# An adaLN block with delta-rule attention and routed experts: half of each inverse root from one ScalarE activation

## The chip, the cores and the metric

The kernel runs on one core of one Trainium2 chip. The metric is the device time of one execution in microseconds (us); lower is better. The core has five engines with a queue of instructions each: TensorE (PE) multiplies matrices, VectorE (DVE), ScalarE (ACT) and GpSimd (POOL) work element by element on 128 partitions, SyncE (SP) issues DMAs. Each engine works its own list in order, and engines wait for each other by semaphores. ScalarE holds one table of functions at a time; where the next activation needs another, a load of a table (`ACT_TABLE_LOAD`) stands in front of it.

## The reference

```python
def step(S, inp):                                    # 256 times, for 16 batches x 16 heads
    qt, kt, vt, at, bt = inp
    Sd = at[..., None, None] * S
    u = vt - jnp.einsum('bhk,bhkv->bhv', kt, Sd)
    Sn = Sd + bt[..., None, None] * kt[..., None] * u[:, :, None, :]
    return (Sn, jnp.einsum('bhk,bhkv->bhv', qt, Sn))
...
k = k * jax.lax.rsqrt(jnp.sum(k * k, -1, keepdims=True) + 1e-12)      # root of the keys
o = o * jax.lax.rsqrt(jnp.mean(o * o, -1, keepdims=True) + 1e-6)      # root of the outputs
...
h = _layernorm(x, axis=-1) * (1 + ca) + sa           # root of the variances, 1e-5
x = x + ga * attention(h)
h = _layernorm(x, axis=-1) * (1 + cb) + sb           # root of the variances, 1e-5
x = x + gb * experts(h)                              # best of 8 experts per row, silu(a) * g @ w2
```

x is 16 x 256 x 128, all in fp32, with heads of 8 values. Every inverse square root in it is one of three kinds: of the variances of rows (layer norm), of the squared length of each key, of the mean square of each output.

## The kernel before, in words

Time is cut into two slices of 128 steps, and batches into two halves of 8. Sequences (batch, head) lie on the 128 partitions of a half `h`; the recurrence is worked in 64 chunks of 4 steps.

Front (0 to 81 us of the profile): VectorE takes statistics of x and scales the rows (`normalise`), TensorE turns and projects them in eight blocks, ScalarE evacuates each block (`shift`, `evacuate`), SP and POOL move them by DMA onto the partitions of their sequences, and VectorE prepares the first slice: unit keys, decay factors, a triangular solve per chunk (`key_norms`, `unit_keys`, `decay_factors`, `key_products`, `substitute`).

Scan (81 to 345 us): VectorE runs four instructions per chunk and half (L1479, L1485, L1492, L1498). Between them it works, one step at a time, through a Python generator, `between()`: the preparation of the second slice, then the first slice's output norm, second layer norm, router and sort. Every `yield` of the generator gives way to one instruction of the scan; `after_chunk(n)` holds it until chunk n. ScalarE's own work for the same things is tied to chunk numbers too. POOL makes products of queries and states, which TensorE sums.

Experts (345 to 543 us): 46 tiles of 128 sorted rows, 23 for each slice. Tile g's weights are copied by ScalarE (`copy_w1`, L1219), TensorE computes the hidden rows (L718) and the outputs (L733), ScalarE applies Silu (L1206), VectorE the gate (`gate_u`, L1695). The second slice's output norm, attention projection, layer norm, router and sort are done beside the first slice's tiles, at fixed g (`F_ATTEND`, `F_ROOT`, `F_TURN`, `F_ROUTE`). POOL scatters the second slice's rows (L868) before tile 23 can start, and scatters each tile's result (L921).

An inverse root has two engines. VectorE makes the argument with its epsilon (`variances` L1309, `key_norms` L1350, `sums_of_squares` L1507) and posts `root_in`; ScalarE's `root` takes the square root by `ACT.Sqrt` (L947) and posts `root_out`; VectorE takes the reciprocal and one Newton step (`rsqrt` L1290 to L1293; for the keys, whose argument, root and result lie in PSUM, `unit_keys` L1357 to L1361 with a copy to SBUF). `settle` makes each wait for the one before. There are ten such roots: four of variances on 128x16 values, four of keys on 128x128, two of outputs on 128x256. An eleventh `ACT.Sqrt` at L1231, whose result nobody uses, stands before the first copies of weights.

Of the kernel before, what the change touches and what calls it, by code (L numbers as in the profile page):

```python
# [12 lines left out]
P = 128  # L13
# [5 lines left out]
def adaln_block(nc, x, Wq, Wk, Wv, Wo, Wbet, Wf, norm_w, router_w, router_b, w1, w2, c, wmod, out):  # L19
# [66 lines left out]
    with ExitStack() as ctx:  # L86
# [56 lines left out]
        ve = sb("ve", [P, NT])  # L143
        sd = sb("sd", [P, NT])
# [618 lines left out]
        def _(pool):  # L763
# [89 lines left out]
            def place_rows(s):  # L853
                for h in range(NHALF):
                    if s == 0:
                        pool.wait_ge(sem("prod_ready", h), NG // 2 + 1)
                    else:
                        pool.wait_ge(sem("sqo_used"), 2)
# [71 lines left out]
        def _(act):  # L930
# [13 lines left out]
            def root(dst, src):  # L944
                roots[0] += 1
                act.wait_ge(sem("root_in"), roots[0])
                act.activation(dst, src, ACT.Sqrt).then_inc(sem("root_out"), 1)  # L947
# [49 lines left out]
            def key_roots(h, s):  # L997
                vectors = bank_vectors(h, s)
                root(vectors[1], vectors[0])

            root(sd[:, :], ve[:, :])
# [4 lines left out]
            root(sd[:, :], ve[:, :])  # L1006
# [90 lines left out]
            def squares(s, h):  # L1097
# [7 lines left out]
                act.activation(SQO[s][h], K_[h][:, s * P:(s + 1) * P, :], ACT.Square).then_inc(sem("sqo"), 1)  # L1105
# [21 lines left out]
            def rows(k):  # L1127
# [3 lines left out]
                if k == 4:  # L1131
                    act.wait_ge(sem("sqo_used"), 2)
# [19 lines left out]
            for n in range(NCH):  # L1152
# [30 lines left out]
                if n == AT_ROOT:  # L1183
                    root(sm[:, 3, :], sm[:, 2, :])
                if n == AT_ROWS:
                    root(sd[:, :], ve[:, :])
# [44 lines left out]
            act.activation(sd[:, :], ve[:, :], ACT.Sqrt)  # L1231
# [5 lines left out]
            root(sm[:, 3, :], sm[:, 2, :])  # L1237

            for g in range(G):
# [9 lines left out]
                if g == F_ROOT:  # L1249
                    root(sd[:, :], ve[:, :])  # L1250
# [5 lines left out]
        def _(dve):  # L1256
# [29 lines left out]
            def rsqrt(var, sroot, y, t):  # L1286
# [3 lines left out]
                yield from settle(dve.reciprocal(y, sroot))  # L1290
                yield from settle(dve.tensor_tensor(t, y, y, ALU.mult))
                yield from settle(dve.scalar_tensor_tensor(out=t, in0=t, scalar=-0.5, in1=var, op0=ALU.mult, op1=ALU.mult))
                dve.scalar_tensor_tensor(out=y, in0=t, scalar=1.5, in1=y, op0=ALU.add, op1=ALU.mult).then_inc(sem("roots_ready"), 1)  # L1293
# [11 lines left out]
            def variances():  # L1305
                for t in range(NT):
                    last = dve.bn_aggr(mv[:, t, :], st[:, t, :])
                yield from settle(last)
                yield from ask_root(dve.tensor_scalar(ve[:, :], mv[:, :, 1], LN_EPS, None, ALU.add))  # L1309
# [8 lines left out]
            def normalise(s):  # L1318
# [4 lines left out]
                now(rsqrt(ve[:, :], sd[:, :], yy[:, :], y2[:, :]))  # L1323
# [19 lines left out]
            def key_norms(h, s):  # L1343
# [5 lines left out]
                yield from settle(dve.tensor_reduce(n2, slice_rows(K_[h], s), AX_X, ALU.add))  # L1349
                yield from ask_root(dve.tensor_scalar(n2, n2, K_EPS, None, ALU.add))  # L1350

            def unit_keys(h, s):
                beta, a, n2, rt, rn, t_, d2, d3 = slice_vectors(h, s)
                n2, rt, rn, a = bank_vectors(h, s)
                count = roots[0]
                dve.wait_ge(sem("root_out"), count)
                yield from settle(dve.reciprocal(rn, rt))  # L1357
                yield from settle(dve.tensor_copy(d2, rn))
                yield from settle(dve.tensor_tensor(t_, rn, d2, ALU.mult))
                yield from settle(dve.scalar_tensor_tensor(out=t_, in0=t_, scalar=-0.5, in1=n2, op0=ALU.mult, op1=ALU.mult))  # L1360
                dve.scalar_tensor_tensor(out=rn, in0=t_, scalar=1.5, in1=rn, op0=ALU.add, op1=ALU.mult).then_inc(sem("roots_ready"), 1)  # L1361
                yield
                dve.wait_ge(sem("roots_ready"), count)
# [136 lines left out]
            def sums_of_squares(s, h):  # L1500
# [3 lines left out]
                if h == 1:  # L1504
                    last.then_inc(sem("sqo_used"), 1)
                    dve.wait_ge(sem("sqo_used"), s + 1)
                    yield from ask_root(dve.tensor_scalar(ms, ms, 1.0 / HD, O_EPS, ALU.mult, ALU.add))  # L1507
# [121 lines left out]
            def first_slice_rows():  # L1629
# [11 lines left out]
                yield from rsqrt(*(sm[:, i, :] for i in (2, 3, 4, 5)))  # L1641
# [170 lines left out]
```

## Time and profile before

| | us |
|---|---|
| median of 3 runs (517.99 to 519.32) | 518.33 |
| profiled execution, first to last instruction (span; the profile gives no other time of it) | 543.5 |
| VectorE busy in it | 414.1 (76%) |
| TensorE busy | 389.4 (72%) |
| GpSimd busy | 276.2 (51%) |
| ScalarE busy | 272.0 (50%) |

The busy share is a mean over stages with different limits. The page puts reciprocals of the keys (L1357) at 3.8 us for 4, reciprocals of the outputs (L1290) at 3.5 us for 2, and loads of ScalarE's table at 1283 ns each, 20 of them. In a row of a timeline stand start, duration, engine, line, operation, output and input tile with shapes, the count of instructions merged into the row, and in brackets the idle time before it and what ended it. A start that follows the end of the row before at once means that nothing was waited for. The mean granted TensorE clock was 0.840 of full speed.

### The profile page before, as it was taken

What the parts mean: (1) busy time and instruction counts of PE and PEld (TensorE: products, weight loads), DVE (VectorE), ACT (ScalarE), POOL (GpSimd) and SP (SyncE); (2) the same over time, 40 slices, a digit from 0 to 9 for tenths busy, and PEclk for the clock granted to TensorE, in tenths of its full rate; (3) what the DMA queues carried; (4) which work ended last, traced back from release to release, by engine and by line L of the source; (5) the groups of instructions that cost most, each with busy time, mean ns of one, the idle gap of its engine ahead of it and who ended that gap; (6) DMA issues with size and microseconds to landing.
All of it is one profiled execution on the core that took longest, in us unless ns stands there. A gap on an engine that the chain in (4) does not pass through costs nothing. (4 is left out here: it accounts for less than half of the span.)

```text
span 543.5 us, 8910 instructions
## 1 busy us (share of the span) xinstructions
PE 389.4 (72%) x2643; PEld 352.1 (65%) x2643; DVE 414.1 (76%) x1196; ACT 272.0 (50%) x600; POOL 276.2 (51%) x323
## 2 busy tenths in 40 slices
PE   2957555969677799450968664879999338999980
PEld 1322115969677699450968663879999238999980
DVE  5679999996999978999998996685957013548733
ACT  2688749663144244554555461453755026555620
POOL 1174329699999674537379375002223743232430
PEclk9988775868977787975889776789999759999996
DMA  8367859900000009203100012024130111233205
GB/s 206 60 70 122 117 105 144 113 1 1 0 2 1 0 8 378 82 0 50 29 2 0 1 35 60 20 39 99 41 107 25 55 54 40 77 91 94 60 29 159
DMA packets 50205, 35.01 MB, mean 64 GB/s; under 512 B 10992, under 2 KB 46608, under 8 KB 50032
## 3 DMA queue, kind: packets, MB, share of 16 engines
q1 hardware_dynamic: 47152, 29.07, 27.5%
q0 software_dynamic: 3008, 5.40, 3.2%
q8 instruction: 22, 0.36, 0.3%
q14 instruction: 23, 0.19, 0.1%
HBM read 15.26 MB, written 10.27 MB: 47 GB/s over the span
## 5 line engine op out<-in xcount | busy, mean ns | idle before, releaser
L570 PE MATMUL bank<-prod_o,ID 128*128 128x128 f32 x512 | 85.5, 336 | 41.3 <-POOL prod_o L287 18.0
L921 POOL DMA_INDIRECT placed_y<-Q,place x46 | 44.1, 958 | 126.0 <-ACT Q L1226 60.6
L570 PEld LDWEIGHTS bank<-prod_o,ID 128*128 128x128 f32 x512 | 79.9, 246 | 43.1 <-POOL prod_o L287 18.8
L718 PE MATMUL bank<-Q,p 128*128 128x128 f32 x736 | 96.5, 280 | 0.0
L718 PEld LDWEIGHTS bank<-Q,p 128*128 128x128 f32 x736 | 91.6, 196 | 0.1
L280 POOL TENSOR_TENSOR prod_o<-Q,ST 128x1024 f32<-128x1024 f32 x28 | 62.5, 2231 | 42.4 <-PE bank L574 29.1
L1063 ACT ACTIVATE p<-S,GAM 128x64 f32<-128x64 f32 x126 | 47.6, 410 | 70.6 <-DVE S L1498 68.0
L1219 ACT ACTIVATE p<-big 128x1024 f32 x46 | 48.5, 1057 | 54.8 <-PE bank L718 36.9
L1498 DVE TENSOR_REDUCE S<-p 128x64 f32<-128x320 f32 x126 | 55.4, 474 | 6.5 <-ACT p L1063 6.0
L1485 DVE TENSOR_REDUCE U<-p 128x32 f32<-128x288 f32 x128 | 52.7, 439 | 0.2 <-DVE p L1479 0.2
L1479 DVE TENSOR_TENSOR p<-S,bank 128x256 f32<-128x256 f32 x128 | 49.2, 407 | 0.7 <-ACT bank L1058 0.7
L1492 DVE TENSOR_TENSOR p<-U,bank 128x256 f32<-128x256 f32 x126 | 47.3, 408 | 0.6 <-DVE U L1485 0.6
L537 PE MATMUL bank<-ph,WP 128*128 128x512 f32 x48 | 32.1, 822 | 18.1 <-ACT ph L959 14.0
L287 POOL TENSOR_TENSOR prod_o<-PD,U 128x128 f32<-128x128 f32 (+1 forms) x112 | 41.5, 405 | 0.0
L1695 DVE TENSOR_TENSOR S<-S,bank 128x512 f32<-128x512 f32 x31 | 21.3, 686 | 25.4 <-PE bank L718 12.5
L574 PEld LDWEIGHTS bank<-prod_o,ID 128*128 128x128 f32 x256 | 37.4, 223 | 3.8 <-issue 3.8
L574 PE MATMUL bank<-prod_o,ID 128*128 128x128 f32 (+3 forms) x256 | 37.1, 293 | 3.4 <-issue 3.4
L1688 DVE COPY Q<-bank 128x128 f32<-128x128 f32 x46 | 13.2, 287 | 33.0 <-PE bank L706 23.9
L868 POOL DMA_INDIRECT sorted_h<-X,pos x32 | 30.8, 963 | 14.1 <-issue 9.1
L733 PE MATMUL bank<-big,S 128*128 x248 | 34.3, 283 | 3.6 <-DVE Q L1702 2.0
L733 PEld LDWEIGHTS bank<-big,S 128*128 128x128 f32 x248 | 30.9, 196 | 4.6 <-issue 4.6
L537 PEld LDWEIGHTS bank<-ph,WP 128*128 128x128 f32 x48 | 11.3, 250 | 32.2 <-ACT ph L959 17.4
(225 smaller groups left out, 786.7 us busy)
## 6 DMA issues: line engine op xcount, KB each, us to landing
big<-in_L_ffn_w_dram SPq DMA_DIRECT2D x1, 4096.0 KB, 13.1
big<-big SPq DMA_DIRECT2D x16, 192.0 KB, 4.5
Q<-sorted_h SPq DMA_DIRECT2D x46, 64.5 KB, 2.0
sorted_h<-ZERO SPq DMA_DIRECT2D x2, 1472.0 KB, 16.4
X<-in_L_attn_x_dram SPq DMA_DIRECT2D x8, 256.0 KB, 4.8
big<-big SPq DMA_DIRECT2D x16, 128.0 KB, 4.9
X<-Q SPq DMA_DIRECT2D x32, 64.0 KB, 2.4
K<-placed_y SPq DMA_DIRECT2D x8, 256.0 KB, 3.0
```

The costliest lines, as they stand in the source:

```text
L280: engine.tensor_tensor(slot[:, 0:HD, :, :, :], q, states.unsqueeze(3).broadcast_to(full), ALU.mult)
L570: pe.matmul(ps, ID[:, :], prod_o[:, k % 2, i, :], start=(i == 0), stop=False, skip_group_check=True)
L574: m = pe.matmul(o4, ID[:, :], r4, start=False, stop=(d == C - 1), skip_group_check=True)
L718: m = pe.matmul(bank[(1, 6)[g % 2] + k][:, c * P:(c + 1) * P], W1E[g % 2][:, f:f + P], XST[:, g % 3, :], start=True, stop=True)
L733: m = pe.matmul(bank[3][:, 0:D], GU[g % 3][:, c * P:(c + 1) * P], W2[:, bass.ds(expert, 1), c, :], start=(c == 0), stop=(c == FC - 1))
L921: pool.indirect_dma_start(placed_y[g // NF], bass.IndirectOffsetOnAxis(ap=place[:, g:g + 1], axis=0), YS[:, g % YR, :], None).then_inc(sem ...
L1063: act.activation(p2[h][:, :, :, C], S_[h][:, n % SR, :, :], ACT.Copy, scale=GAM[h][:, n:n + 1])\
L1219: act.activation(W1E[g % 2].unsqueeze(1), W1[:, bass.ds(expert, 1), :], ACT.Copy).then_inc(sem("w1_copied"), 1)
L1479: dve.tensor_tensor(p1[h][:, n % UR, :, :, 0:HD], s_, w, ALU.mult).then_inc(sem("seq_w", h), 1)
L1485: dve.tensor_reduce(U_[h][:, n % VR, :, :], p1[h][:, n % UR, :, :, :], AX_X, ALU.add)\
L1492: dve.tensor_tensor(p2[h][:, :, :, 0:C], u, k, ALU.mult).then_inc(sem("state_in", h), 1)
L1498: dve.tensor_reduce(S_[h][:, (n + 1) % SR, :, :], p2[h][:, :, :, :], AX_X, ALU.add).then_inc(sem("s_ready", h), 1)
```

## The change

ScalarE no longer gives a square root but `Abs_reciprocal_sqrt` of 4 v + 4 eps, which is half of the inverse root. VectorE keeps a Newton step written for the half: t = -4 half half, t = (v + eps) t, y = (t + 3) half. The epsilon operations, the reciprocals and the keys' copy go. The outputs' 1/8 moves into ScalarE's Square. The reduction itself (or the last aggregation) now posts `root_in`, and two waits on `sqo_used` become waits on a count of `root_in`. The unused `ACT.Sqrt` at L1231 goes. For the keys, `half` lies in SBUF (`d2`), argument and result in PSUM. The diff leaves out the two tiles that go and further calls of `root` and `rsqrt` with their new arguments.

```diff
@@ -855,7 +853,7 @@
                     else:
-                        pool.wait_ge(sem("sqo_used"), 2)
+                        pool.wait_ge(sem("root_in"), 2 * NHALF + 2 * NTIME + 1)
@@ -941,10 +939,11 @@
-            def root(dst, src):
+            def root(half, src, eps):
+
...
                 act.wait_ge(sem("root_in"), roots[0])
-                act.activation(dst, src, ACT.Sqrt).then_inc(sem("root_out"), 1)
+                act.activation(half, src, ACT.Abs_reciprocal_sqrt, scale=4.0, bias=4.0 * eps).then_inc(sem("root_out"), 1)
@@ -995,15 +994,14 @@
             def key_roots(h, s):
-                vectors = bank_vectors(h, s)
-                root(vectors[1], vectors[0])
-
-            root(sd[:, :], ve[:, :])
+                root(slice_vectors(h, s)[6], bank_vectors(h, s)[0], K_EPS)
+
+            root(yy[:, :], mv[:, :, 1], LN_EPS)
...
             evacuate(1)
-            root(sd[:, :], ve[:, :])
+            root(yy[:, :], mv[:, :, 1], LN_EPS)
@@ -1102,7 +1100,8 @@
                         act.wait_ge(sem("q_decayed", hh), 2)
-                act.activation(SQO[s][h], K_[h][:, s * P:(s + 1) * P, :], ACT.Square).then_inc(sem("sqo"), 1)
+                act.activation(SQO[s][h], K_[h][:, s * P:(s + 1) * P, :], ACT.Square, scale=HD ** -0.5)\
+                    .then_inc(sem("sqo"), 1)
@@ -1228,13 +1227,12 @@
-            act.activation(sd[:, :], ve[:, :], ACT.Sqrt)
...
                 squares(1, h)
-            root(sm[:, 3, :], sm[:, 2, :])
+            root(sm[:, 4, :], sm[:, 2, :], O_EPS)
@@ -1283,14 +1281,13 @@
-            def rsqrt(var, sroot, y, t):
+            def rsqrt(var, eps, half, y, t):
...
                 dve.wait_ge(sem("root_out"), count)
-                yield from settle(dve.reciprocal(y, sroot))
-                yield from settle(dve.tensor_tensor(t, y, y, ALU.mult))
-                yield from settle(dve.scalar_tensor_tensor(out=t, in0=t, scalar=-0.5, in1=var, op0=ALU.mult, op1=ALU.mult))
-                dve.scalar_tensor_tensor(out=y, in0=t, scalar=1.5, in1=y, op0=ALU.add, op1=ALU.mult).then_inc(sem("roots_ready"), 1)
+                yield from settle(dve.scalar_tensor_tensor(out=t, in0=half, scalar=-4.0, in1=half, op0=ALU.mult, op1=ALU.mult))
+                yield from settle(dve.scalar_tensor_tensor(out=t, in0=var, scalar=eps, in1=t, op0=ALU.add, op1=ALU.mult))
+                dve.scalar_tensor_tensor(out=y, in0=t, scalar=3.0, in1=half, op0=ALU.add, op1=ALU.mult).then_inc(sem("roots_ready"), 1)
@@ -1305,8 +1302,7 @@
                     last = dve.bn_aggr(mv[:, t, :], st[:, t, :])
-                yield from settle(last)
-                yield from ask_root(dve.tensor_scalar(ve[:, :], mv[:, :, 1], LN_EPS, None, ALU.add))
+                yield from ask_root(last)
@@ -1346,21 +1342,12 @@
                 dve.wait_ge(sem("ksq"), NHALF * s + h + 1)
-                yield from settle(dve.tensor_reduce(n2, slice_rows(K_[h], s), AX_X, ALU.add))
-                yield from ask_root(dve.tensor_scalar(n2, n2, K_EPS, None, ALU.add))
+                yield from ask_root(dve.tensor_reduce(n2, slice_rows(K_[h], s), AX_X, ALU.add))
...
                 n2, rt, rn, a = bank_vectors(h, s)
-                count = roots[0]
-                dve.wait_ge(sem("root_out"), count)
-                yield from settle(dve.reciprocal(rn, rt))
-                yield from settle(dve.tensor_copy(d2, rn))
-                yield from settle(dve.tensor_tensor(t_, rn, d2, ALU.mult))
-                yield from settle(dve.scalar_tensor_tensor(out=t_, in0=t_, scalar=-0.5, in1=n2, op0=ALU.mult, op1=ALU.mult))
-                dve.scalar_tensor_tensor(out=rn, in0=t_, scalar=1.5, in1=rn, op0=ALU.add, op1=ALU.mult).then_inc(sem("roots_ready"), 1)
-                yield
-                dve.wait_ge(sem("roots_ready"), count)
+                yield from rsqrt(n2, K_EPS, d2, rn, t_)
@@ -1502,9 +1489,7 @@
                 if h == 1:
-                    last.then_inc(sem("sqo_used"), 1)
-                    dve.wait_ge(sem("sqo_used"), s + 1)
-                    yield from ask_root(dve.tensor_scalar(ms, ms, 1.0 / HD, O_EPS, ALU.mult, ALU.add))
+                    yield from ask_root(last)
@@ -1638,14 +1623,14 @@
                 yield from after_chunk(AT_ROOT)
-                yield from rsqrt(*(sm[:, i, :] for i in (2, 3, 4, 5)))
+                yield from rsqrt(sm[:, 2, :], O_EPS, sm[:, 4, :], sm[:, 4, :], sm[:, 5, :])
...
                 yield from after_chunk(AT_ROWS)
-                yield from rsqrt(ve[:, :], sd[:, :], yy[:, :], y2[:, :])
+                yield from rsqrt(mv[:, :, 1], LN_EPS, yy[:, :], yy[:, :], y2[:, :])
```

## Rows read from the trace of the kernel before

**Rows 1.** Busy time of each engine in four stretches (us, instructions), clock, DMA.
```profile
33.00:81.50 48.50, 30.15 (x61) 9.79 (x59) 44.94 (x81) 35.42 (x64) 22.28 (x21) 0.82 0.64 101
...
130.00:180.00 50.00, 39.18 (x264) 38.71 (x263) 49.97 (x117) 16.50 (x54) 49.30 (x48) 0.80 0.00 1
...
380.00:419.00 39.00, 37.05 (x325) 36.06 (x324) 29.40 (x117) 22.95 (x37) 9.58 (x10) 1.00 0.18 57
419.00:444.00 25.00, 6.59 (x47) 5.94 (x45) 2.23 (x8) 2.91 (x4) 16.28 (x17) 0.66 0.19 59
```

**Rows 2.** Timeline of VectorE: the first root of variances.
```profile
10.69 0.17 DVE L1309 TENSOR_SCALAR ve<-RT 128x16 f32<-128x16 f32 x1
11.22 0.25 DVE L1290 RECIPROCAL yy<-sd 128x16 f32<-128x16 f32 x1 [0.36 <-ACT sd L947]
```

**Rows 3.** Timeline of VectorE: second root of variances, first root of keys.
```profile
28.93 0.25 DVE L1290 RECIPROCAL yy<-sd 128x16 f32<-128x16 f32 x1 [5.84 <-ACT sd L947]
...
33.29 1.23 DVE L1349 TENSOR_REDUCE bank<-K 128x128 f32<-128x1024 f32 x1 [1.29 <-ACT K L980]
34.55 0.30 DVE L1350 TENSOR_SCALAR bank<-bank 128x128 f32<-128x128 f32 x1
35.25 0.96 DVE L1357 RECIPROCAL bank<-bank 128x128 f32<-128x128 f32 x1 [0.40 <-ACT bank L947]
...
36.57 0.29 DVE L1359 TENSOR_TENSOR sm<-bank,sm 128x128 f32<-128x128 f32 x1
```

**Rows 4.** Timeline of ScalarE: the second root of keys.
```profile
53.04 1.28 ACT L947 ACT_TABLE_LOAD   x1
55.67 0.26 ACT L947 ACTIVATE bank<-bank 128x128 f32<-128x128 f32 x1 [1.35 <-DVE bank L1350]
```

**Rows 5.** Timelines of POOL, TensorE and VectorE: from the front into the scan.
```profile
81.50 6.04 POOL L827 TENSOR_TENSOR prod_o<-Q,K 128x1024 f32<-128x1024 f32 x4 [7.62 <-DVE X L1436]
...
87.60 10.64 PE L590 MATMUL bank<-prod_o,ID 128*128 128x128 f32 x64 [10.60 <-POOL prod_o L827]
...
128.74 0.26 DVE L1418 TENSOR_TENSOR sm<-sm,bank 128x96 f32<-128x96 f32 x1 [4.15 <-PE bank L603]
```

**Rows 6.** Timeline of VectorE: reciprocals inside the scan, and what follows each.
```profile
136.98 0.95 DVE L1357 RECIPROCAL bank<-bank 128x128 f32<-128x128 f32 x1
137.84 0.39 DVE L1485 TENSOR_REDUCE U<-p 128x32 f32<-128x288 f32 x1
...
243.52 1.75 DVE L1290 RECIPROCAL sm<-sm 128x256 f32<-128x256 f32 x1
245.18 0.36 DVE L1479 TENSOR_TENSOR p<-S,bank 128x256 f32<-128x256 f32 x1
...
274.44 0.61 DVE L1309 TENSOR_SCALAR ve<-RT 128x16 f32<-128x16 f32 x1
```

**Rows 7.** Timeline of ScalarE, where the experts start.
```profile
345.92 1.28 ACT L1231 ACT_TABLE_LOAD   x1
...
351.30 1.06 ACT L1105 ACTIVATE X<-K 128x1024 f32<-128x1024 f32 x1
...
354.40 1.28 ACT L1206 ACT_TABLE_LOAD   x1
```

**Rows 8.** Timeline of VectorE, the same stretch.
```profile
353.64 0.29 DVE L1507 TENSOR_SCALAR sm<-sm 128x256 f32<-128x256 f32 x1
...
355.01 1.74 DVE L1290 RECIPROCAL sm<-sm 128x256 f32<-128x256 f32 x1
356.79 0.42 DVE L1291 TENSOR_TENSOR sm<-sm 128x256 f32<-128x256 f32 x1
...
358.17 0.69 DVE L1695 TENSOR_TENSOR S<-S,bank 128x512 f32<-128x512 f32 x1
```

**Rows 9.** Timelines of TensorE and ScalarE: a late transfer, and a standstill.
```profile
368.75 2.05 PE L619 MATMUL bank<-ph,X 128*128 128x128 f32 x16 [1.02 <-DMA X<-Q]
...
441.44 1.06 ACT L1219 ACTIVATE p<-big 128x1024 f32 x1 [12.03 <-remote]
```

More of the change, by code:

```diff
@@ L142, in adaln_block @@
         mv = RT[:, 992:1024].rearrange("p (t a) -> p t a", t=NT)
-        ve = sb("ve", [P, NT])
-        sd = sb("sd", [P, NT])
         yy = sb("yy", [P, NT])
@@ L1131, in rows @@
                 if k == 4:
-                    act.wait_ge(sem("sqo_used"), 2)
+                    act.wait_ge(sem("root_in"), 2 * NHALF + 2 * NTIME + 1)
                 act.activation(H2[s][q // 2][:, q % 2 * 4:q % 2 * 4 + 4, 0:D], BACK_BANKS[s][q][:, :].rearrange("p (n d) -> p n d", n=4), ACT.Copy)\
@@ L1183, in _ @@
                 if n == AT_ROOT:
-                    root(sm[:, 3, :], sm[:, 2, :])
+                    root(sm[:, 4, :], sm[:, 2, :], O_EPS)
                 if n == AT_ROWS:
-                    root(sd[:, :], ve[:, :])
+                    root(yy[:, :], mv[:, :, 1], LN_EPS)
                 if n in AT_STATS:
@@ L1236, in _ @@
                 squares(1, h)
-            root(sm[:, 3, :], sm[:, 2, :])
+            root(sm[:, 4, :], sm[:, 2, :], O_EPS)
             for g in range(G):
@@ L1249, in _ @@
                 if g == F_ROOT:
-                    root(sd[:, :], ve[:, :])
+                    root(yy[:, :], mv[:, :, 1], LN_EPS)
                 if g == NF - 1:
@@ L1322, in normalise @@
                 now(variances())
-                now(rsqrt(ve[:, :], sd[:, :], yy[:, :], y2[:, :]))
+                now(rsqrt(mv[:, :, 1], LN_EPS, yy[:, :], yy[:, :], y2[:, :]))
                 scale(s, tile, XN[s], "xn_ready", range(HB if s else NT))
@@ L1740, in _ @@
                 if g == 0:
-                    now(rsqrt(*(sm[:, i, :] for i in (2, 3, 4, 5))))
+                    now(rsqrt(sm[:, 2, :], O_EPS, sm[:, 4, :], sm[:, 4, :], sm[:, 5, :]))
                 if g - 1 in F_ATTEND:
@@ L1753, in _ @@
                 if g == F_ROOT + 1:
-                    now(rsqrt(ve[:, :], sd[:, :], yy[:, :], y2[:, :]))
+                    now(rsqrt(mv[:, :, 1], LN_EPS, yy[:, :], yy[:, :], y2[:, :]))
                     scale(1, second_tile, XNB, "xn2_ready", range(NT // 2))
```

## The prediction

> **What bounds the kernel now.** I read the busy time by stretch first, because the page's busy shares mix stages. VectorE is busy 44.94 of 48.5 us in the second part of the front and 49.97 of 50 in the middle of the scan; POOL is busy 49.30 of the same 50; between 380 and 419 us TensorE is the full one (37.05 of 39) [rows 1]. So an instruction that leaves VectorE should shorten the span up to about 345 us, unless a wait already stands behind it, and should be worth little beside the experts' tiles. Then I went through VectorE's timeline for its idle times, as each is a place where an earlier saving can stop. Up to 345 us those that matter are: 5.84 us for ScalarE's second root and 1.29 us for the keys' squares [rows 3], and 4.15 us at 128.74 for TensorE's sums of key products [rows 5]. Last I followed the two other engines at the start of the experts [rows 7, 8] and looked for what stops all of them at once [rows 9].
>
> **The front.** First root of variances: without L1309 the argument is ready 10.89 - 10.69 = 0.20 us earlier (its 0.17 us and a gap), and the reciprocal goes (0.25 us and a gap of 0.04) [rows 2]. The Newton step is three instructions before and after, on operands of the same shape, so it costs the same. 0.20 + 0.29 = 0.49 us, and all that follows (turning, projecting, moving the keys) hangs on these rows. Second root of variances: VectorE waits 5.84 us for ScalarE, which is in its own queue behind the projections, so L1309 is worth nothing; the reciprocal's 0.29 us comes back, but is lost at 33.29, where VectorE waits 1.29 us for the squares of the keys [rows 3]. Counted: 0.
>
> First root of keys: L1350 takes 34.55 to about 34.88, 0.33 us; from the reciprocal to L1359 it is 36.57 - 35.25 = 1.32 us, which holds the reciprocal (0.96) and the copy that goes [rows 3]. What remains is a product, and the two instructions of the step. Saved 1.65 us. The second root of keys in the front has the same five instructions, so 1.65 us again, if its root is there in time. ScalarE waited 1.35 us for VectorE before it, with the table long loaded (53.04 to 54.32) [rows 4]. VectorE now has the argument 0.49 + 1.65 + 0.33 = 2.47 us sooner, so ScalarE is the later one, at about 54.3 less 0.5; VectorE wants the result some 3 us after that. No loss. The front gives 0.49 + 3.30 = 3.79 us.
>
> Whether this reaches the scan is the first choice I had to make. At 128.74 VectorE waits for TensorE, and the chain behind that is TensorE's sums of query products from 87.60 on, begun by POOL's products at 81.50, which waited 7.62 us for VectorE's last substitution [rows 5]. So the wait at 128.74 moves with the front: 3.79 us pass through. But what is saved between 82 and 128 us (the third root of keys, the fourth's epsilon) only makes the wait of 4.15 us longer. Counted: 0.
>
> **The scan.** Here the generator puts each removed instruction between two of the recurrence, and they overlap a little: the reciprocal of 0.95 us moves its successor by 137.84 - 136.98 = 0.86 us, the one of 1.75 us by 245.18 - 243.52 = 1.66 us [rows 6]. Fourth root of keys: 0.86 and a copy, for which I take 0.2 (it is of the shape of L1350, 0.30 us in [rows 3], less the same overlap of 0.1): 1.06 us. First root of outputs: 1.66 and an epsilon operation of 0.2 (0.29 alone in [rows 8], less 0.1): 1.86 us. Third root of variances: L1309 took 0.61 us there [rows 6], and a short reciprocal, 0.25 less 0.1: I count 0.5. ScalarE's waits in this part lead back to TensorE and POOL, and these back to chunks that VectorE had finished; so all of it passes. 1.06 + 1.86 + 0.5 = 3.42 us.
>
> POOL is nearly as full as VectorE from 130 to 180 us [rows 1], which speaks against this; the bounds are 0 (POOL sets the pace) and 3.42. I take 3.42, because the run of POOL ends in an idle stretch that waits for TensorE, not for POOL's own work.
>
> **The start of the experts.** The unused Sqrt at L1231 goes, with its 1.28 us load [rows 7], but a load has to stand somewhere: it now comes before the root itself, after the square that ends at 351.30 + 1.06 = 352.36. A load is not held back by the wait of the activation that it is for (1.35 us of waiting stand behind the load of [rows 4]), so it runs from 352.36 to 353.65. VectorE's last sum ends at about 353.61 (before L1507 at 353.64) and no longer needs the epsilon operation, so the root starts at about 353.68, against 353.96: nearly hidden, and 0.28 us earlier. VectorE then needs 3 x 0.46 = 1.38 us instead of 1.78 + 3 x 0.46 (from L1290 to L1291 is 356.79 - 355.01 = 1.78) [rows 8]. The tile's gate at L1695 waits for the step and for Silu, whose load at 354.40 [rows 7] moves by 0.28. Gate: 358.17 less about 2.0 us, 356.1 to 356.2. The scaling of outputs, its transfer and the projection for which TensorE waited 1.02 us at 368.75 [rows 9] follow it. I take 2.0; the bounds are 1.02 (only that wait goes) and 2.06 (1.78 + 0.28). With the cover gone, a load costs 1.28 us there: were it issued only with the root, the sum would be 2.0 - 1.3 = 0.7.
>
> A rule to weigh against this: the row has the load at 1.28 us, and the engine busy again at once behind it [rows 7]. The Trainium skill, "ScalarE: Activation LUTs", section "What ACT_TABLE_LOAD costs", charges a switch at about 2.66 us, a load and a drain of 1.38 us. With the drain the moved load would end 1.4 us behind the sum, and 0.6 us would be left of the 2.0; the trace shows no such drain, and I go by the trace.
>
> **Beside the tiles.** The last root of variances gives at most 0.49 us by the first one's rows; TensorE is full there, and I count 0.2.
>
> **What could be added.** The activation itself: 0.26 us for Sqrt on 128x128 [rows 4]; the new function is not in the trace. Square on 1024 elements takes 1.06 us [rows 7] and Sqrt on 128 0.26: an activation goes by its elements. Below, the new one costs the same; above, I allow twice that for each of the five on the path, 5 x 0.26 = 1.3 us. I take the same. The count of loads: Copy, Identity and Square run between a Sqrt and the next load in this trace, and I take it that they stand in the new function's table too. The Square's scale costs nothing by the form of the instruction.
>
> **Sum.** 3.79 + 3.42 + 2.0 + 0.2 = 9.4 us. The profiled span would be 543.5 - 9.4 = 534.1. That span is 25.2 us longer than the median of 518.33; I can't place the difference, but the standstill below is as long. The instructions saved are the same either way, so I take 9.2 from the median, a little less for gaps that open: 509.1 us.
>
> **The rivals.** A. Another engine takes over inside the scan: POOL at 49.30 of 50 us [rows 1]. Then the front's 3.79 us and the last 2.2 us stay, less some, and the scan's 3.4 goes: 518.3 - 5.8 = 512.5. For it: POOL's share; against it: the 7.62 us that POOL waited for VectorE [rows 5].
>
> B. The standstill moves. Between 419 and 444 us, while POOL issues the second slice's scatters, TensorE, VectorE and ScalarE are busy for 6.59, 2.23 and 2.91 of 25 us [rows 1], and ScalarE waits 12.03 us for nothing that the profile can name [rows 9]. If this depends on where in its list each engine is, 20 instructions fewer can change it. Worse: one more such wait of 12.03 us on the path, and the kernel is slower, 518.3 - 9.2 + 12.0 = 521.1; it decides from 9.2 us on. Better: the some 8 us of tiles that now run after it fit under POOL's scatters: 509.1 - 8 = 501.
>
> C. The new function's table lacks Copy, Identity or Square. Then up to ten more loads of 1.28 us, 12.8 us on ScalarE, of which I would expect a third on the path: 509.1 + 4.3 = 513.4. All ten on the path would make 521.9.
>
> D. The gain is there only in part because the moved load is not hidden and the second stretch of the front has a new wait: 509.1 + 1.3 + 1 = 511.4. This lies in my forecast's own range of 506.5 to 511.5.
>
> **Chances.** Forecast with D 0.63, A 0.16, B worse 0.06, B better 0.10, C 0.05. The range from 503.5 to 514.0 holds the forecast, A, most of C and a part of B better. 0.3% is 1.6 us, the least that can be told from no change: faster 0.90, same 0.04, slower 0.06.
>
> **What would show it.** In the changed profile: 20 loads of tables as before; no reciprocal of 0.96 or 1.74 us; the key products' wait (4.15 us before) at about 125.0 and longer, some 5.6 us; the scan's end 7.2 us earlier; the first gate of the experts 9.2 us earlier than 358.17; the last root's load covered by the sum of squares. I am wrong if VectorE shows new idle time between 33 and 81 us or for POOL in the scan, if ScalarE's loads are more than 20, or if the first gate is early and the end is not, which would be the standstill.

## The result, and the profile after

The changed kernel takes 512.34 us (median of 4 runs, 511.5 to 515.14), the kernel before beside it 518.83 us (4 runs, 517.99 to 521.38). The ratio is 0.9887, 95% interval 0.9848 to 0.9926: 5.9 us faster, from 3.8 to 7.9 (the medians alone differ by 6.5). I had forecast 9.2 us less and 509.1 us.

The profiled execution of the changed kernel has a span of 509.7 us (its time 511.5), that of before 543.5. These 34 us are not the change. The windows of the changed kernel (window, length, busy us of TensorE, its weight loads, VectorE, ScalarE and POOL with instruction counts, granted clock, DMA share, GB/s) answer to [rows 1]:

```profile
33.00:80.50 47.50, 28.44 (x60) 9.54 (x58) 44.30 (x75) 35.31 (x64) 22.68 (x21) 0.82 0.73 104
130.00:180.00 50.00, 39.57 (x261) 39.12 (x260) 49.97 (x108) 16.59 (x54) 49.02 (x47) 0.79 0.00 1
...
419.00:444.00 25.00, 23.16 (x199) 22.34 (x198) 11.07 (x34) 15.13 (x20) 17.22 (x18) 1.00 0.39 112
```

The last row shows that this execution has no standstill. Every later comparison was run on one of three other chips, where each kernel shows it and takes some 27 us more (the kernel before 545.1 to 546.3 us). There I compare times only by the ratio to the kernel before beside them. Traces can be set side by side across these chips: from 201 to 214 us, where VectorE never waits, two kernels on two chips run alike to 0.01 us.

The first two rows show what didn't happen: in the scan's stretch VectorE starts nine instructions fewer, of which the change removed only two there (a reciprocal and a copy), and is busy for the same 49.97 of 50 us. Over the whole execution it went from 414.1 to 411.0 us, 3.1 us, while the reciprocals, epsilon operations and copies that go were busy for 12.4 us by the groups of the kernel before (3.8 + 3.5 + 1.0 of reciprocals, 1.2 + 1.1 + 0.6 of epsilons, 1.2 of copies). So something else got longer. The groups by form name most of it (busy us, mean ns of one):

```profile
L1288 DVE SCALAR_TENSOR_TENSOR sm<-sm 128x128 f32<-128x128 f32 x2 | 3.3, 1668 | 0.4 <-ACT sm L946 0.4
L1290 DVE SCALAR_TENSOR_TENSOR bank<-XN 128x128 f32<-128x128 f32 x2 | 3.0, 1484 | 0.0
L1289 DVE SCALAR_TENSOR_TENSOR sm<-bank,sm 128x128 f32<-128x128 f32 x2 | 0.6, 282 | 0.0
```

Three steps of the same form and size; the two whose inputs both lie in SBUF take five to six times as long in the mean. The mean hides a spread: of the eight steps of this kind (L1288 and L1290 at four roots of keys) three are long, 3.00, 1.62 and 1.35 us, and five take 0.28 to 0.34. The three long ones account for 5.1 of the 9.3 us that are missing. Another 2.3 us are in older instructions with two SBUF inputs, which the change left alone: the products of keys with keys (`multiply_pairs`, big<-K, "the pairs" below) went from 5.3 to 6.4 us busy, and the substitutions of the triangular solve (L1421 and L1423) from 35.1 to 36.3. In the scan, instructions overlap by about 0.1 us each, which a sum over groups counts twice. The timelines of VectorE and of POOL, put side by side at the third root of keys and then at the second and fourth, say why:

```profile
94.23 3.00 DVE L1288 SCALAR_TENSOR_TENSOR sm<-sm 128x128 f32<-128x128 f32 x1
...
97.48 0.28 DVE L1289 SCALAR_TENSOR_TENSOR sm<-bank,sm 128x128 f32<-128x128 f32 x1
...
98.04 0.28 DVE L1290 SCALAR_TENSOR_TENSOR bank<-sm 128x128 f32<-128x128 f32 x1
...
92.56 2.59 POOL L794 TENSOR_TENSOR X<-big,sm 128x1024 f32<-128x1024 f32 x1
95.11 1.96 POOL L842 TENSOR_TENSOR Q<-Q,sm 128x1024 f32<-128x1024 f32 x1
```

```profile
59.16 1.62 DVE L1290 SCALAR_TENSOR_TENSOR bank<-XN 128x128 f32<-128x128 f32 x1
...
137.19 1.35 DVE L1290 SCALAR_TENSOR_TENSOR bank<-XN 128x128 f32<-128x128 f32 x1
...
58.55 2.07 POOL L811 TENSOR_TENSOR big<-K,sm 128x1024 f32<-128x1024 f32 x1 [9.64 <-DVE X L1423]
...
136.16 2.22 POOL L278 TENSOR_TENSOR prod_o<-Q,ST 128x1024 f32<-128x1024 f32 x1
```

VectorE's step ends at 97.23, 60.78 and 138.54; POOL's instruction ends at 97.07, 60.62 and 138.38. Each time it is 0.16 us, so the step can finish only when POOL is through. No wait stands in the profile, only a long duration: that a row which follows the one before at once has waited for nothing, as said ahead of the rows, does not hold for such an instruction. In the kernel before, all instructions of a root of keys read at most one operand from SBUF, since argument and root lay in PSUM. The change put `half` into SBUF.

The Trainium skill, "SBUF — State Buffer", section "Who interferes with whom", states this: a VectorE instruction with two SBUF inputs and a GpSimd instruction that reads SBUF share a read path, whoever issues first holds it, and the other blocks fully. The rows above agree. My prediction did not weigh it.

VectorE's other rows at the places of the prediction, and ScalarE's at the start of the experts:

```profile
28.77 0.17 DVE L1288 SCALAR_TENSOR_TENSOR y<-yy 128x16 f32<-128x16 f32 x1 [6.58 <-ACT yy L946]
...
33.10 1.23 DVE L1345 TENSOR_REDUCE bank<-K 128x128 f32<-128x1024 f32 x1 [1.57 <-ACT K L979]
...
126.84 0.26 DVE L1405 TENSOR_TENSOR sm<-sm,bank 128x96 f32<-128x96 f32 x1 [1.81 <-PE bank L601]
...
241.66 0.41 DVE L1288 SCALAR_TENSOR_TENSOR sm<-sm 128x256 f32<-128x256 f32 x1
...
243.03 0.40 DVE L1290 SCALAR_TENSOR_TENSOR sm<-sm 128x256 f32<-128x256 f32 x1
...
343.46 0.42 DVE L1288 SCALAR_TENSOR_TENSOR sm<-sm 128x256 f32<-128x256 f32 x1
...
344.86 0.69 DVE L1680 TENSOR_TENSOR S<-S,bank 128x512 f32<-128x512 f32 x1
```

```profile
340.07 1.06 ACT L1103 ACTIVATE X<-K 128x1024 f32<-128x1024 f32 x1
341.15 1.28 ACT L946 ACT_TABLE_LOAD   x1
342.44 0.42 ACT L946 ACTIVATE sm<-sm 128x256 f32<-128x256 f32 x1
342.88 1.28 ACT L1205 ACT_TABLE_LOAD   x1
```

The last root of outputs takes no longer by the new function (0.42 us, as by Sqrt), and tables are loaded 20 times, as before. From the last square's end to the first gate it is 344.86 - 341.13 = 3.73 us, against 358.17 - 352.36 = 5.81 in [rows 7, 8].

### The profile page after: what moved, and what is told of

It reads as the page before. It is cut to its first block, busy times and chain, and to the rows that moved or that the text cites. A ratio compares the mean times of both kernels' runs of the same rounds, so it can differ in the third digit from the quotient of the medians.

```text
span 509.7 us, 8886 instructions
## 1 busy us (share of the span) xinstructions
PE 382.6 (75%) x2643; PEld 346.9 (68%) x2643; DVE 411.0 (81%) x1172; ACT 272.2 (53%) x599; POOL 277.2 (54%) x323
## 4 chain that ended last, share of the span: by engine, by line
DVE 39%; PE 38%; issue 8%; POOL 6%; DMA 4%; ACT 2%; SPq 2%; ACTq 0%; POOLq 0%; DVEq 0%
PE bank L716 11%; PE bank L568 7%; PE bank L731 5%; PE bank L588 5%; DVE U L1472 5%; DVE S L1485 4%; DVE p L1479 4%; DVE p L1466 4%; DVE big L1421 3%; DVE X L1423 3%; PE bank L572 2%; POOL placed_y L919 1%; PE bank L601 1%; DVE big L1391 1%; PE bank L535 1%
## 5 line engine op out<-in xcount | busy, mean ns | idle before, releaser
L568 PE MATMUL bank<-prod_o,ID 128*128 128x128 f32 x512 | 84.4, 333 | 39.9 <-ACT K L1091 16.9
L568 PEld LDWEIGHTS bank<-prod_o,ID 128*128 128x128 f32 x512 | 78.7, 242 | 41.4 <-issue 17.6
L716 PE MATMUL bank<-Q,p 128*128 128x128 f32 x736 | 94.8, 277 | 0.0
L716 PEld LDWEIGHTS bank<-Q,p 128*128 128x128 f32 x736 | 89.8, 193 | 0.2
L572 PEld LDWEIGHTS bank<-prod_o,ID 128*128 128x128 f32 x256 | 37.2, 223 | 0.0
L588 PE MATMUL bank<-big,ID 128*128 128x128 f32 (+3 forms) x192 | 31.8, 340 | 1.0 <-POOL big L825 1.0
```

The source lines that it names most:

```text
L568: pe.matmul(ps, ID[:, :], prod_o[:, k % 2, i, :], start=(i == 0), stop=False, skip_group_check=True)
L572: m = pe.matmul(o4, ID[:, :], r4, start=False, stop=(d == C - 1), skip_group_check=True)
L588: m = pe.matmul(ps, ID[:, :], t4[:, :, :, k], start=(k == 0), stop=(k == HD - 1))
L716: m = pe.matmul(bank[(1, 6)[g % 2] + k][:, c * P:(c + 1) * P], W1E[g % 2][:, f:f + P], XST[:, g % 3, :], start=True, stop=True)
```

## The experiments

Each row of this table is from 5 to 12 timed executions, beside 17 of the kernel before on the same chip.

| kernel | chip | median (range), us | kernel before | ratio, 95% interval |
|---|---|---|---|---|
| changed | first | 539.22 (538.63 to 541.78) | 546.02 | 0.9889 (0.986 to 0.9918) |
| keys padded | first | 543.83 (543.18 to 545.65) | 546.02 | 0.9967 (0.9951 to 0.9983) |
| half twice | first | 541.11 (538.34 to 542.49) | 546.02 | 0.9908 (0.9876 to 0.994) |
| keys as before | second | 539.4 (538.03 to 541.68) | 546.32 | 0.9876 (0.985 to 0.9902) |
| outputs padded | second | 544.76 (543.73 to 546.58) | 546.32 | 0.9978 (0.9959 to 0.9996) |
| new order | second | 539.75 (536.96 to 542.11) | 546.32 | 0.986 (0.983 to 0.9889) |
| half twice, new order | second | 538.43 (536.24 to 542.11) | 546.32 | 0.9848 (0.9809 to 0.9888) |
| changed | third | 539.84 (538.86 to 540.83) | 545.06 | 0.9906 (0.9885 to 0.9928) |
| half twice, new order | third | 536.95 (536.77 to 541.56), 5 runs | 545.06 | 0.986 (0.9834 to 0.9885) |
| before, new order | third | 544.93 (540.3 to 548.09) | 545.06 | 0.9998 (0.9975 to 1.002) |
| root's table early | third | 538.89 (538.35 to 540.59) | 545.06 | 0.9897 (0.9874 to 0.992) |

**The kernel before, and the changed one, on one chip.** 

> The kernel before once more, unchanged, for its trace. Theory S (the two standstills of its first trace, about 4 us at 334 to 338 and about 22 us at 420 to 443, belong to that one execution): the span comes out near 517 us, and from 419 to 444 us TensorE is busy for far more than 6.6 us. Rival (they belong to the kernel, and the change removes them): the span is near 543 us again.

> The changed kernel unchanged, as the point of comparison for the two beside it. Expected 511 to 513 us, a ratio of 0.985 to 0.991 to the kernel before; key steps of VectorE at L1288 and L1290 again stretched from 0.28 us to 1.3 to 3.0 us in three of eight places.

The control took 546.25 us, span 544.5, so my theory S was wrong. But the changed kernel has the standstill here as well (its execution took 541.78 us), so its rival was wrong too: the change does not remove it. Four of the eight steps are long this time, 1.62, 1.08, 1.18 and 1.35 us. Both kernels stand still between 419 and 444 us: in order, the changed one and the one before:

```profile
419.00:444.00 25.00, 7.76 (x41) 7.30 (x41) 2.92 (x10) 3.87 (x5) 14.60 (x16) 0.60 0.18 55
```
```profile
419.00:444.00 25.00, 6.65 (x56) 6.11 (x54) 2.90 (x10) 2.94 (x4) 17.18 (x18) 0.75 0.20 62
```

So the standstill is a matter of the chip or the execution, not of the kernel, and the gain is the same with it and without (0.9887, and 0.9889 in the table). These two traces, of one chip, give the account by place. The starts of the same VectorE instructions, in us:

| VectorE starts | before | changed | keys padded | keys as before |
|---|---|---|---|---|
| first squares of keys are summed | 33.57 | 33.62 | 33.33 | 33.17 |
| first key product (its root is done) | 37.83 | 36.28 | 37.84 | 37.43 |
| decay factors (after the pairs) | 43.20 | 42.64 | 42.55 | 42.45 |
| second key product | 62.84 | 61.34 | 63.68 | 61.48 |
| third key product | 99.48 | 98.06 | 101.65 | 98.12 |
| chunk 16 of the scan | 156.57 | 155.76 | 159.80 | 155.55 |
| chunk 40, behind the outputs' root | 250.20 | 247.43 | 249.57 | 246.08 |
| chunk 48, behind the variances' root | 278.23 | 274.35 | 276.69 | 272.99 |
| last chunk | 342.48 | 338.92 | 341.92 | 336.07 |
| first gate | 359.19 | 353.33 | 356.31 | 350.31 |

Two things in these columns belong to the execution and not to the kernel. The trace of the changed kernel is of the slowest of its six executions (541.78 us), that of the keys as before of the fastest (538.03). And ahead of the last chunk, from 328 to 340 us, VectorE stands idle several times for nothing that the profile can name, in one piece for 3.56, 1.78, 5.30 and 1.80 us.

**Keys padded.** The new form stays, and an epsilon operation, a reciprocal and a copy whose results nobody reads come back:

```diff
+                yield from settle(dve.tensor_scalar(rn, n2, K_EPS, None, ALU.add))
+                yield from settle(dve.reciprocal(rn, n2))
+                yield from settle(dve.tensor_copy(rn, n2))
                 yield from rsqrt(n2, K_EPS, d2, rn, t_)
```

> The changed kernel, with what it took from VectorE per root of keys put back as work that nobody uses: an epsilon operation, a reciprocal and a copy on 128x128 from PSUM to PSUM, 1.6 us each time, ahead of the steps. The outputs and the variances keep the new form. My prediction's terms: 1.65 twice and 1.06, so 4.4 us slower than the changed kernel. Theory P (most of the keys' saving was lost in waiting for POOL's reads): 1 to 2.5 us slower, because padding takes up time in which VectorE would wait anyway.

It is 4.6 us slower than the changed kernel, as the prediction's 4.4 had it, and not the 1 to 2.5 us of the other theory. On this run alone my account of the keys would have passed as confirmed. Its trace is less clear: it is 4.0 us behind the changed kernel's at chunk 16, but only 2.1 at chunk 40, as two waits of VectorE for ScalarE, near 200 and 215 us, take 3.05 us and nothing in it, 3.69 and 1.49 in the other.

**Half twice.** ScalarE writes the keys' half into SBUF and into the bank, so that each step reads one operand of SBUF at most:

```diff
+                act.activation(bank_vectors(h, s)[1], bank_vectors(h, s)[0], ACT.Abs_reciprocal_sqrt, scale=4.0, bias=4.0 * K_EPS)\
+                    .then_inc(sem("half_in"), 1)
...
-                yield from settle(dve.scalar_tensor_tensor(out=t, in0=half, scalar=-4.0, in1=half, op0=ALU.mult, op1=ALU.mult))
+                yield from settle(dve.scalar_tensor_tensor(out=t, in0=half, scalar=-4.0, in1=twin, op0=ALU.mult, op1=ALU.mult))
```

> ScalarE writes the half of the keys' inverse root twice, to PSUM and to SBUF, so that none of VectorE's three steps on keys has two inputs in SBUF. Theory P (such an instruction can't run beside a POOL instruction that reads SBUF, and waits to its end): L1288 at 94 us falls from 3.0 us to 0.28, L1290 at 59 and 137 us from 1.6 and 1.35 to 0.29; of that the one at 94 us lies in the shadow of the wait for the key products, the one at 59 us is lost again on the pairs of keys behind it, which have two inputs in SBUF, so the time falls by 0 to 1.5 us against the changed kernel. Rival Q (the stretch is POOL's and TensorE's pace, or a wait that the trace hides in the duration): the three stay stretched and the time is the same. ScalarE pays 4 x 0.26 us.

The steps are short now, at the place where one took 1.62 us, and the pairs behind them take the wait over (62.98: 3.54 us for three that take 2.14 undisturbed, at 63.61 in the keys as before):

```profile
60.05 0.29 DVE L1292 SCALAR_TENSOR_TENSOR XN<-XN,bank 128x128 f32<-128x128 f32 x1
60.37 0.29 DVE L1293 SCALAR_TENSOR_TENSOR XN<-bank,XN 128x128 f32<-128x128 f32 x1
60.69 0.29 DVE L1294 SCALAR_TENSOR_TENSOR bank<-XN,bank 128x128 f32<-128x128 f32 x1
61.02 1.92 DVE L1356 TENSOR_TENSOR K<-big,bank 128x1024 f32<-128x1024 f32 x1
62.98 3.54 DVE L1396 TENSOR_TENSOR big<-K 128x768 f32<-128x768 f32 x3
```

All twelve steps at the four roots take 0.27 to 0.30 us. The mechanism is confirmed and the cure is not: 541.11 against 539.22 us, with overlapping ranges, where I expected 0 to 1.5 us less. Freed at one instruction, VectorE stops at the next that reads two operands from SBUF while POOL works.

**Keys as before.** The whole of the keys' old form, in the changed kernel:

```diff
+                yield from ask_root(dve.tensor_scalar(n2, n2, K_EPS, None, ALU.add))
...
+                yield from settle(dve.reciprocal(rn, rt))
+                yield from settle(dve.tensor_copy(d2, rt))
+                yield from settle(dve.tensor_tensor(t_, rt, d2, ALU.mult))
+                yield from settle(dve.scalar_tensor_tensor(out=t_, in0=t_, scalar=-4.0, in1=n2, op0=ALU.mult, op1=ALU.mult))
...
```

> The changed kernel with VectorE's work on the roots of the keys put back as it was, at the four places where a root of keys is taken: ScalarE writes its half into the bank alone, VectorE adds the epsilon in an operation of its own, takes a reciprocal (which nothing reads), copies the half, and the three instructions of the step each read at most one operand from SBUF. Variances and outputs keep the new form. By my prediction's terms this gives back 1.65 + 1.65 + 1.06 = 4.4 us, so the kernel is 4.4 us slower than the changed one. By the shared-read theory (the changed form saves instructions at the keys, but makes two of the three steps read two operands from SBUF, and these stand still beside POOL) it is 0 to 1 us slower only. A padded kernel that kept the two-operand steps and added the instructions was 4.6 us slower than the changed one: if this one is too, the placing of the operands is worth nothing.

Ratio 0.9876 against 0.9889 of the changed kernel: the same. By the two intervals the undone kernel is 0.7 us faster, give or take 2.1, so the 4.4 us of the forecast are excluded and a gain of about 1.4 us is not. So all that the change did to the keys, three VectorE instructions of six gone at four places, gained nothing that can be measured. The timeline of VectorE at the first root, in the changed kernel and in this one, and of the padded one at the second:

```profile
35.26 0.33 DVE L1288 SCALAR_TENSOR_TENSOR sm<-sm 128x128 f32<-128x128 f32 x1 [0.41 <-ACT sm L946]
...
36.28 1.92 DVE L1351 TENSOR_TENSOR K<-big,bank 128x1024 f32<-128x1024 f32 x1
38.24 4.37 DVE L1391 TENSOR_TENSOR big<-K 128x768 f32<-128x768 f32 x3
```
```profile
35.13 0.97 DVE L1353 RECIPROCAL bank<-bank 128x128 f32<-128x128 f32 x1 [0.40 <-ACT bank L946]
...
37.43 1.91 DVE L1360 TENSOR_TENSOR K<-big,bank 128x1024 f32<-128x1024 f32 x1
39.38 3.04 DVE L1400 TENSOR_TENSOR big<-K 128x768 f32<-128x768 f32 x3
```
```profile
61.47 2.18 DVE L1290 SCALAR_TENSOR_TENSOR bank<-XN 128x128 f32<-128x128 f32 x1
63.68 1.92 DVE L1355 TENSOR_TENSOR K<-big,bank 128x1024 f32<-128x1024 f32 x1
```

The changed kernel has its root 1.15 us sooner, though it summed its squares 0.45 us later, and the pairs end at 42.61 against 42.42 us: of 1.6 us gained 0.26 are left. The pairs are instructions with two SBUF inputs (2.14 us for the three undisturbed), and POOL's weighing of values lies across them, which itself is held up by them, by the timeline of POOL in the changed kernel and in this one:

```profile
38.48 3.12 POOL L794 TENSOR_TENSOR X<-big,sm 128x1024 f32<-128x1024 f32 x1
```
```profile
37.88 2.53 POOL L794 TENSOR_TENSOR X<-big,sm 128x1024 f32<-128x1024 f32 x1
```

At the second root the step at 59.69 takes 1.62 us and gives the gain back at once (61.34 against 61.48), at the third two steps take 1.08 and 1.18 us (98.06 against 98.12), and at the fourth a lead of 0.8 us (139.48 against 140.26) is gone by chunk 16; what took it there was not tried. The padded kernel pays for both: the added instructions and the long step, 2.18 us in the last fence, at its second root.

**Outputs padded.** An epsilon operation and a reciprocal, whose results nobody reads, stand ahead of both roots of outputs:

```diff
+                yield from settle(dve.tensor_scalar(sm[:, 5, :], sm[:, 2, :], O_EPS, None, ALU.add))
+                yield from settle(dve.reciprocal(sm[:, 5, :], sm[:, 2, :]))
...
```

> The changed kernel with an epsilon operation and a reciprocal on 128x256 elements, whose results nothing reads, ahead of both roots of outputs (one in the scan, one at the start of the experts). By my prediction's terms 1.86 + 2.0 = 3.9 us slower than the changed kernel. If the first is swallowed in the scan by POOL's pace (the prediction's rival A), 2.0 us slower; if the table load moved by the change really hides the second, the same 2.0 stays in the first alone, about 1.9 to 2.2.

By the ratios it is 0.9978 - 0.9889 = 0.0089 of 546.3, 4.9 us slower than the changed kernel (5.4 slower than the keys as before beside it); the prediction had 3.9. In its trace, against the changed kernel, it is 0.92 us ahead at chunk 36 and 0.88 behind at chunk 40, 1.8 us for the scan's root, and from the last sum of squares to the first gate it is 357.58 - 353.02 = 4.56 us against 353.33 - 350.85 = 2.48, 2.1 us. Both terms stand at their place. The 1.0 us beyond them is within the intervals, which allow 1.9 either way.

**Two changes of order.** VectorE takes the first half's decay factors ahead of its pairs, and POOL weighs the second values before it waits for the first keys' factors; alone in the changed kernel, with the half twice, the latter again, and alone in the kernel before:

```diff
-                now(multiply_pairs(h))
-                now(decay_factors(h, 0))
+                for part in ((decay_factors(h, 0), multiply_pairs(h)) if h == 0 else (multiply_pairs(h), decay_factors(h, 0))):
+                    now(part)
...
+            weigh_values(1, 0)
             pool.wait_ge(sem("prep_done", 0), 1)
             decay_keys(0, 0)
-            weigh_values(1, 0)
```

> The changed kernel with two changes of order in the front, no change in what is computed: VectorE takes the decay factors of the first half ahead of the pair products (an instruction with two operands in SBUF, which took 2.91 us beside POOL and 0.69 alone), and POOL weighs the second values before it waits for the first keys' factors. Shared-read theory: of the 2.2 us lost at the pairs in each of two slices a half comes back, 1 to 3 us faster than the changed kernel. If what POOL holds up only moves to the next two-operand instruction, 0 (within 1 us). If POOL's work set the front, its new order alone gives up to 1 us.

> As the one with the two changes of order, and ScalarE writes the half of the keys' roots twice, once into SBUF and once into the bank, so that every instruction of the step reads one operand from SBUF at most. Shared-read theory: the key steps no longer stand still beside POOL (1.3 and 2.7 us twice in the changed kernel) and the pairs don't take the loss over, so 2 to 4 us faster than the changed kernel. If the loss only moves on to later two-operand instructions, as it did with the second half alone (ratio to before 0.9908 against 0.9889), within 1 us of it. ScalarE's four more activations of 0.27 us could cost 0 to 0.5.

> The changed kernel again, as the measure for the three that run beside it: 0.9889 of the kernel before, as it was on another chip, that is about 6 us faster.

> The version with the keys' half written twice and the two changes of order, again, now on one chip with the changed kernel. If its 0.9848 was no chance, it is 1.5 to 3 us faster than the changed kernel here; if it was (the times of this kernel lie in two clusters 3 us apart), within 1 us of it.

> The kernel before with the two changes of order alone (decay factors ahead of the pairs, POOL's second weighing ahead of its first wait). In it all five key steps read at most one SBUF operand, and the lock falls on the pairs (2.04 us instead of 0.69). Shared-read theory: 0.5 to 2 us faster than the kernel before. If the orders only help where the changed steps stand, within 0.5 us of it.

The order alone is 0.986, 1.6 us ahead of the changed kernel's 0.9889 on another chip, with overlapping intervals; that neither shows nor excludes the 1 to 3 us of the theory. The half twice with it is 0.9848 and on the third chip 0.986, where the changed kernel has 0.9906: 2.9 us between the medians, and intervals that meet at 0.9885. So this version has the lowest ratios here, some 2 to 3 us ahead of the changed kernel and 8 ahead of the one before, and not separable from the new order alone.

That the long steps were its cause is not shown, and the traces speak against it: the held instruction has only changed again. The pairs of the first half are short now (2.14 us), but with the new order alone a step of the second root is held twice, and with the half twice the pairs behind it (the third row, from the third chip):

```profile
58.65 2.60 DVE L1288 SCALAR_TENSOR_TENSOR XN<-XN 128x128 f32<-128x128 f32 x1
...
61.62 1.62 DVE L1290 SCALAR_TENSOR_TENSOR bank<-XN 128x128 f32<-128x128 f32 x1
```
```profile
63.09 4.42 DVE L1396 TENSOR_TENSOR big<-K 128x768 f32<-128x768 f32 x3
```

All three traces reach chunk 16 behind the changed kernel's 155.76 us (157.12, 156.08 and 157.01), and at the first gate one is 0.5 us ahead of it (352.85), the others behind. They are of executions that took 542.11, 541.07 and 541.56 us, longer than the medians, so where the medians' 2 to 3 us come from stays open. In the kernel before the order gives nothing in the mean (my 0.5 to 2 us were wrong), with a wide scatter, 540.3 to 548.09.

**The moved table load.** The unused activation comes back, and with it the early load:

```diff
+            act.activation(y2[:, :], mv[:, :, 1], ACT.Abs_reciprocal_sqrt, scale=4.0, bias=4.0 * LN_EPS)
```

> The changed kernel with the unused activation put back ahead of the copy of the weights at the experts' start, so that the root's table is loaded early again, as before. By my prediction the load that now stands directly ahead of the last root lies beside the last sum of squares: 0 to 0.3 us slower than the changed kernel (ScalarE has one activation more). If the moved load is not hidden, up to 1.3 us faster.

538.89 against 539.84 us, the same within their ranges; I had expected 0 to 0.3 us more, and the times alone don't tell that from a load that is not hidden. The rows do. ScalarE's timeline in the changed kernel on that chip, then in this one:

```profile
346.64 1.06 ACT L1103 ACTIVATE X<-K 128x1024 f32<-128x1024 f32 x1
347.71 1.28 ACT L946 ACT_TABLE_LOAD   x1
349.00 0.42 ACT L946 ACTIVATE sm<-sm 128x256 f32<-128x256 f32 x1
```
```profile
346.05 1.06 ACT L1103 ACTIVATE X<-K 128x1024 f32<-128x1024 f32 x1
348.39 0.42 ACT L946 ACTIVATE sm<-sm 128x256 f32<-128x256 f32 x1 [1.29 <-DVE sm L1491]
```

From the square's end to the root it is 1.30 us with the load between and 1.29 with VectorE's sum alone: the load fills the wait exactly, as worked out from [rows 7, 8].

## Why the prediction was right and where it was wrong

The total lies within the stated range of 503.5 to 514.0, 3.2 us above the forecast value. It is outside the band of 506.5 to 511.5 that I gave the forecast itself, and that it is inside the range is in part luck: of the 9.2 us, the 4.4 for the keys were not there, which a wide range and smaller terms with the other sign hide. None of the signs named beforehand (new idle time of VectorE, more than 20 loads, an early first gate without an early end) points at the fault, because the lost time stands in durations.

- **Roots of keys, 3.30 us in the front and 1.06 in the scan: wrong, about 0.** The step that failed is "What remains is a product, and the two instructions of the step": I priced the new steps by the old ones' 0.29 us without looking at where their operands lie. Two of the three now read both from SBUF; beside POOL they took 3.00, 1.62 and 1.35 us at three of the four roots, and the one root where they are short (35 us) runs into the pairs, which POOL holds anyway. The undone form is as fast (0.9876 against 0.9889).
- **First root of variances, 0.49 us: there at its place, lost behind it.** From the start of the last aggregation to the first scaled row it is 2.65 us in the three traces with the old form and 2.16 or 2.17 in the eleven with the new one, 0.49 as forecast. But in the first pair of traces TensorE begins to turn the rows 0.68 us earlier (12.62 against 13.30), its first six projections then take 5.42 instead of 4.90 us, and ScalarE's second root comes 0.17 us earlier only. In the second pair x arrived later in the changed kernel, and both are level at 33.6 us (33.57, 33.62). Over all traces the squares of the keys are summed at 32.60 to 33.81 us in the new form and 33.29 to 33.93 in the old, so the term can't be told there. The changed kernel enters the scan 1.2 us ahead; of that 0.66 us is a wait of the kernel before for POOL, which its trace has and that of [rows 1 to 5] has not.
- **The pass from 82 to 128 us: the place was right, the sign not.** I wanted the wait of 4.15 us at 125.0 and at 5.6 us; it is at 126.84 and 1.81 us (127.29 and 2.77 in the second trace). The saving that should have made it longer was eaten at 94.23.
- **First root of outputs, 1.86 us: right.** From chunk 16 to chunk 40 the lead grows from 0.81 to 2.77, 1.96 us, and padding costs 1.8 at its place.
- **Third root of variances, 0.5 us: too small**, 3.88 - 2.77 = 1.1 us. Of this, 0.43 us is a wait of VectorE for ScalarE ahead of the statistics, at 265.64 us in the kernel before (0.40 at 264.68 in its first trace); both traces of the changed kernel lack it. I had not counted it.
- **Start of the experts, 2.0 us: right.** 5.81 - 3.73 = 2.08 us in the first pair of traces; the padded kernel pays 2.1. The load was hidden, with no drain, as the row had it against the rule that I weighed.
- **Rivals.** A has the measured number (512.5 forecast, 512.3 measured), and that is chance: it kept the front's 3.79 us and gave up the scan's 3.42, while the runs show the front's 3.30 for the keys gone and 1.96 + 1.1 of the scan's there. POOL does limit, but as holder of the read path and not by a pace of its own. B: the standstill does not follow the kernel. C: no; 20 loads. D: the load is hidden.
- **Checks named beforehand.** The scan's end came 3.6 us earlier (7.2 forecast) and the first gate 5.9 (9.2), by the two traces of one chip. 4.8 of the 5.9 us are left behind the standstill, at about 460 us, and 4.4 at the last gate; where the rest went was not tried. The 5.9 us are 0.8 up to chunk 16, 1.96 and 1.1 in the scan and 2.3 from the last chunk to the gate, less 0.3 at the scan's end.

## What to carry to other kernels

A removed instruction pays only up to the next point at which its engine must stop, and one such point is no wait in the profile: an instruction with two SBUF inputs beside a working POOL. Before pricing a new instruction by an old one of the same form and size, compare where each input lies, and look whether its duration has a spread. And take a term back by undoing the code, not only by padding the new form: here padding "confirmed" 4.6 us where undoing showed none, within 2.1 us.

## What the runs showed of the hardware

- The block on the shared read path is whole and lasts to the end of POOL's instruction, 0.16 us after it in three cases, through two POOL instructions back to back in one (94.23, 3.00 us). POOL suffers the same when VectorE comes first: L794 took 3.12 us where the pairs had begun 0.24 us before it (38.24 and 38.48), and 2.53 where it had begun 1.5 us before them (37.88 and 39.38), the pairs then taking 3.04.
- TensorE's granted clock decides 1.3 us in the scan. Between 212 and 215 us it was granted at half (1.2 GHz) in the changed kernel on the first chip and mostly at full in the kernel with the keys as before, after the same work (TensorE was busy without a pause from 200 us on); VectorE's wait behind it is 1.49 and 0.16 us:

```profile
212.00:215.00 3.00, 3.00 (x17) 3.00 (x15) 2.50 (x8) 0.00 (x0) 0.00 (x0) 0.50 1.02 412
```
```profile
212.00:215.00 3.00, 3.00 (x26) 3.00 (x26) 2.84 (x9) 0.95 (x4) 0.00 (x0) 0.90 1.02 399
```

- The times of several of these kernels lie in two clusters some 3 us apart (the changed one 538.6 to 539.5 and 541.6 to 541.8). That wait near 215 us goes with them in part. Of the five traces in which it is 0.16 us or missing, three are of the shortest execution of their kernel in that run (511.5, 538.03, 540.3 us) and one of the second shortest (538.6); of the nine in which it is 1.43 to 1.52 us, five are of the longest or second longest of a kernel's executions (541.78, 542.11, 541.56, 541.07, 541.4). It is worth 1.3 of the 3 us at most; the rest stays open, as does the cause of the standstill.
